# A four-layer gated stack on one core: layer 0's value product in fp32 over centred values, biases added by two-row matmuls, high parts written by ScalarE

## The reference

```python
x = x + tanh(g_xattn[0]) * L0_xattn(layernorm(x), ctx, ctx)   # 8 heads of 16, decay gates
x = x + tanh(g_ffn[0])   * L0_ffn(layernorm(x))               # 8 experts, top 2, capacity 320
x = x + tanh(g_xattn[1]) * (layernorm(x) @ W1.T + mean(ctx) @ W2.T + b)
x = x + tanh(g_ffn[1])   * L1_ffn(layernorm(x))               # rounded to 16 and 4 bits
x = x + tanh(g_xattn[2]) * L2_xattn(layernorm(x), ctx)        # two attentions, 16 heads of 8
x = x + tanh(g_ffn[2])   * L2_ffn(layernorm(x))               # 8 experts, top 2
x = x + tanh(g_xattn[3]) * L3_xattn(layernorm(x), ctx)        # one attention, 16 heads of 8
x = x + tanh(g_ffn[3])   * L3_ffn(layernorm(x))               # 8 experts and a shared one
```

```python
# L0_xattn, per head (16 columns)
C      = (q @ k.T) * exp(D - max_d) / 4
H      = (C @ v) / (max(|sum(C)|, exp(-max_d)) + 1e-6)
out    = (H - mean(H)) / sqrt(var(H) + 1e-5) * gn_w + gn_b     # mean and var over the head's 16
# L2_xattn: x is the normalised input, c the context
a = ln(x + relu(mha1(x, x, x) @ Wo1 + bo1)) * g1 + b1          # causal
c = ln(2 * relu(mha2(ctx, ctx, a) @ Wo2 + bo2)) * g2 + b2
y = ln(c + relu(c @ Wf + bf)) * g3 + b3
```

## Time and profile before

| | us |
|---|---|
| median of 3 runs | 606.84 (605.1 to 607.8) |
| the profiled execution, its own time | 607.42 |
| its span | 605.5 |
| DVE busy | 461.4 |
| PE busy | 420.0 |
| ACT busy | 308.2 |
| POOL busy | 234.4 |

### The profile page before, as it was taken

The page is one execution under the profiler, slowest core; times in us unless marked ns, Lnnn a source line. Parts: engine busy times, 40 slices in busy tenths (PEclk is TensorE's granted clock), DMA queues, the critical chain, the costliest instruction groups (busy, mean ns, idle before and its releaser), DMA issues.

```text
span 605.5 us, 11360 instructions
## 1 busy us (share of the span) xinstructions
PE 420.0 (69%) x4079; PEld 273.0 (45%) x4079; DVE 461.4 (76%) x1305; ACT 308.2 (51%) x596; POOL 234.4 (39%) x358
## 2 busy tenths in 40 slices
PE   2575341258999548103999978776589997878895
PEld 2543220135666433002556656554255664666532
DVE  5559999875667875687978888999878679796742
ACT  2476652227555323732556736762456554757641
POOL 4527775629557670631110111135355572121100
PEclk9999655559999867656999978976799998796988
DMA  7830000450000000000000000000000000000000
GB/s 222 172 32 2 1 1 0 157 122 2 2 1 1 2 0 1 1 0 1 1 2 2 2 1 2 2 2 1 1 2 1 2 0 3 1 2 2 1 17 18
DMA packets 26838, 11.86 MB, mean 20 GB/s; under 512 B 16056, under 2 KB 23712, under 8 KB 26784
## 3 DMA queue, kind: packets, MB, share of 16 engines
q1 hardware_dynamic: 26784, 11.14, 7.4%
HBM read 10.61 MB, written 0.52 MB: 18 GB/s over the span
## 4 chain that ended last, share of the span: by engine, by line
DVE 43%; PE 39%; POOL 6%; issue 6%; ACT 5%; DMA 1%; SPq 1%; DVEq 0%; ACTq 0%
PE psum L653 10%; PE psum L818 6%; DVE qs L1614 5%; PE psum L803 3%; PE psum L804 3%; PE psum L805 3%; DVE stats L1192 3%; DVE z L1200 2%; POOL work L614 2%; PE psum L990 2%; DVE at L1503 1%; DVE mv L1194 1%; PE psum L926 1%; PE psum L930 1%; DVE split L1364 1%
## 5 line engine op out<-in xcount | busy, mean ns | idle before, releaser
L536 POOL TENSOR_SCALAR vr<-mv 128x1 f32<-128x1 f32 x88 | 19.4, 220 | 217.6 <-DVE mv L1194 217.3
L614 POOL TENSOR_TENSOR work<-work 128x512 f16<-128x512 f32 x64 | 72.6, 1162 | 43.2 <-ACT work L1066 43.2
L1614 DVE TENSOR_REDUCE qs<-psum 128x4 f16<-128x512 f32 x96 | 59.6, 689 | 6.0 <-PE psum L905 5.8
L1008 ACT ACTIVATE phase<-psum 128x1024 f16<-128x1024 f16 (+1 forms) x52 | 47.5, 928 | 30.5 <-PE psum L891 15.2
L1491 DVE TENSOR_TENSOR work<-work,psum 128x512 f32<-128x512 f32 x64 | 42.9, 685 | 20.3 <-ACT work L1112 19.8
L1112 ACT ACTIVATE work<-psum 128x512 f32<-128x512 f32 x64 | 37.5, 594 | 37.2 <-PE psum L805 34.5
L1153 ACT ACTIVATE phase<-psum 128x512 f32<-128x512 f32 x96 | 49.8, 601 | 9.5 <-PE psum L930 8.8
L538 POOL TENSOR_TENSOR rstd<-vr,mhalf 128x1 f32<-128x1 f32 x88 | 50.1, 570 | 7.3
L803 PE MATMUL psum<-zTh,split 128*128 128x512 f16 x128 | 51.1, 399 | 1.9 <-DVE work L1491 1.5
L818 PE MATMUL psum<-wout,work 128*128 128x128 f16 x768 | 48.9, 223 | 3.3 <-POOL work L614 1.8
L804 PE MATMUL psum<-zTl,split 128*128 128x512 f16 x128 | 51.0, 398 | 0.0
(11 more groups left out here) (347 smaller groups left out, 1040.1 us busy)
## 6 DMA issues: line engine op xcount, KB each, us to landing
stage_f<-in_L_ffn_W_in SPq DMA_DIRECT2D x1, 2048.0 KB, 10.0
stage_f<-in_L_ffn_w SPq DMA_DIRECT2D x1, 2048.0 KB, 8.4
x<-in_x SPq DMA_DIRECT2D x1, 512.0 KB, 4.1
c<-in_ctx SPq DMA_DIRECT2D x1, 512.0 KB, 5.5
...
```

The costliest lines, as they stand in the source:

```text
L614: ch.do(pool.tensor_tensor(hidl[:, n % 2, k, :], act[:, n % 2, k, :], hidh[:, n % 2, k, :], ALU.subtract), sem("hid_low"))
L1008: ch.do(A(out, view(u), ACT.Copy), banks.freed(stage, b, name))
L1614: ch.do(v.tensor_reduce(groups(qs[:, b, :, 3 * DA:3 * DA + 1], 4)[:, j], u, AX.X, ALU.max, negate=True), free_of(stage, b, f"s{j}"))
```

## The change

- **Layer 0.** Stage x0_cut is gone. dec stays in fp32 and is the moving operand; the values are the weights of the matmul, 32 columns for a head, in fp32, with the mean over each head's 16 columns taken off before (cm). x0_value now gives the result transposed; ACT copies it (avT0), PE transposes it back in a new stage x0_back, ACT takes its squares, and DVE has five steps left. The mean needs no step, since the values are centred, and the division by the norm is folded into the power: it is taken of var + 1e-5 * norm^2. POOL adds gn_b (scaled by tanh(g)) to x ahead, so that x0_group has three steps.
- **Biases by matmul.** Eight bias rows are loaded on two partitions (bias32, in the load group "l2"), ACT takes their fp16 high parts in stage w1, POOL makes the two rows of bias16 in stage router, and PE opens an accumulation with minus16 (all -1) times bias16 (add_bias): in x1_out, c_kv, b_q, a_wo, b_wo and b_f. A b_q bias comes from b1 times Wq2, in w1, and g1 is multiplied into Wq2, so that a_norm is the plain normalising step.
- **High parts on ScalarE.** In m_kv and b_q, ACT writes both high parts and the values; DVE writes the low parts alone (low).
- **Norms.** b_norm and b_last are two steps (affine). POOL adds b3 and bo (scaled) to x behind x2_z and x3_z.
- **Loads.** 7 rows on 128 partitions in the place of 13, none for bq, bk and bv; in "l2" come seven loads on two partitions, g1 and b1 twice.

```diff
-    "x0": ["x0_split", "x0_stack", "x0_score", "x0_cut", "x0_value", "x0_group", "f0_z", "f0_t"],
+    "x0": ["x0_split", "x0_stack", "x0_score", "x0_value", "x0_back", "x0_group", "f0_z", "f0_t"],
-    "x0_split": 12.8, "x0_stack": 13.8, "x0_score": 14.8, "x0_cut": 15.8, "x0_value": 16.8, "x0_group": 17.8,
+    "x0_split": 12.8, "x0_stack": 13.8, "x0_score": 14.8, "x0_value": 15.8, "x0_back": 16.8, "x0_group": 17.8,
-    "setup": ["ctx0", "ctx1", "gate_w"], "w1": ["u"], "w8": ["u"], "router": ["u"],
+    "setup": ["ctx0", "ctx1", "gate_w"], "w1": ["u", "bq"], "w8": ["u"], "router": ["u"],
...
@@ POOL @@
-                    ch.do(pool.tensor_tensor(v0[:, b, :, D0 + 1:2 * D0 + 1], cb, kk[:, :, 0:D0], ALU.subtract), sem("v0_ready"))
-                elif stage == "x0_cut":
...
+                    if b == 0:
+                        pool.wait_ge(sem("cm_ready"), 1)
+                    ch.do(pool.tensor_tensor(v0[:, b, 0:H0 * n0].rearrange("p (h d) -> p h d", h=H0)[:, :, 0:D0], cb,
+                                             bc(cm[:, b * H0:(b + 1) * H0].unsqueeze(2), [P, H0, D0]), ALU.subtract), sem("v0_ready"))
...
+                    ch.do(pool.tensor_tensor(x[:, b, :], x[:, b, :], vec("L0_xattn_gn_b"), ALU.add), sem("x_biased"))
...
+                elif stage == "router":
+                    loaded(pool, "rows")
+                    pool.wait_ge(sem("tg_ready"), 1)
+                    for name, k in (("L2_xattn_g3", 2), ("L2_xattn_b3", 2), ("L3_xattn_bo", 3)):
+                        ch.do(pool.tensor_scalar(rows_of(name), rows_of(name), tg[:, k:k + 1], None, ALU.mult),
+                              sem("rows_scaled") if k == 3 else None)
+
+                    pool.wait_ge(sem("bias_high"), 1)
+                    ch.do(pool.tensor_scalar(bias16[:, :, :], bias16[:, :, :], ident[0:2, 1:2], None, ALU.mult))
+                    ch.sync()
+                    ch.do(pool.tensor_tensor(bias16[:, :, :], bias16[:, :, :], bias32, ALU.subtract), sem("bias_ready"))
+                    ch.do(pool.tensor_scalar(wB[:, 0, :], wB[:, 0, :], g1c[:, :], None, ALU.mult), sem("wq_scaled"))
@@ PE @@
+            def add_bias(out, first, n=1):
+
+                return mm_(out, minus16[:, :], bias16[:, first:first + n, :].rearrange("p i d -> p (i d)"), start=True, stop=False)
...
-                    for h in range(H0):
-                        mm_(u[:, h * n:(h + 1) * n], ch0[:, b % 2, h, :], v0[:, b, h, :], start=True, stop=False)
-                        last = mm_(u[:, h * n:h * n + D0 + 1], cl0[:, b % 2, h, :], v0[:, b, h, 0:D0 + 1], start=False, stop=True)
+                    for g in range(2):
+                        banks.emptied(pe, "x0_score", b, f"s{g}")
+                        for j in range(4):
+                            h = 2 * j + g
+                            last = one(u[32 * j:32 * j + SLOTA, g * P:(g + 1) * P], v0[:, b, h * n0:h * n0 + SLOTA], dec[:, b % 2, g, j, :])
+                    banks.fill(last, stage, b, "u")
+                elif stage == "x0_back":
+                    banks.emptied(pe, "x0_value", b, "u")
+                    u = banks.take(pe, stage, b, "u")
+                    for g in range(2):
+                        last = tr(u[:, g * P:(g + 1) * P], avT0[:, b % 2, g, :], ident[:, :])
@@ ACT @@
+                    u = banks.get(act_, stage, b, "bq")
+                    ch.do(A(bias32[:, 7, :], u[0:2, 0:D], ACT.Copy), banks.freed(stage, b, "bq"))
+                    act_.wait_ge(*banks.freed(stage, b, "bq"))
+                    loaded(act_, "l2")
+                    ch.do(A(bias16[:, :, :], bias32, ACT.Copy), sem("bias_high"))
...
+                elif stage in ("a_kv", "b_kv", "c_kv"):
...
+                    if m != "b":
+                        twice(qs[:, b, :, 0:2 * DA].rearrange("p h (s d) -> p h s d", d=DA), heads(u[:, 0:D]))
+                    twice(ks[:, b, :, 0:4 * DA].rearrange("p h (s d) -> p h s d", d=DA)[:, :, 0:3:2, :], heads(u[:, D:2 * D]))
+                    ch.do(A(vA[:, b, :, 0:DA], heads(u[:, 2 * D:3 * D]), ACT.Copy), sem(m + "_kv_high"))
@@ DVE @@
+            def affine(stage, out, src, b, tmp, gain, plus, signal):
+
+                dve.wait_ge(sem("rstd_ready"), norm_turn[NORM_OF[stage], b])
+                ch.do(stt(tmp, src, mv[:, b, 0:1], gain, ALU.subtract, ALU.mult))
+                ch.sync()
+                ch.do(stt(out, tmp, rstd[:, b:b + 1], plus, ALU.mult, ALU.add), signal)
...
+                elif stage == "x0_gate":
+                    if b == NB - 1:
+                        ch.do(v.tensor_reduce(cm[:, :], c[:, :, :].rearrange("p b (h d) -> p (b h) d", d=D0), AX.X, ALU.add))
...
-                        ch.do(tt(w, u[:, 0:3 * D].rearrange("p (i d) -> p i d", i=3), bqkv[:, :, :], ALU.add), f)
...
+                    dve.wait_ge(sem(m + "_kv_high"), b + 1)
+                    u = banks.tile(stage, b, "qkv")
+                    if m != "b":
+                        low(b, u[:, 0:D], 0)
+                    low(b, u[:, D:2 * D], 1, free_of(stage, b, "qkv"))
```

More of the change, by code:

```diff
@@ L680, in _ @@
                     banks.fill(last, stage, b, "u")
+                    loaded(pe, "l2")
+                    u = banks.take(pe, stage, b, "bq")
+                    banks.fill(one(u[0:2, 0:D], b1c[:, :], wB[:, 0, :]), stage, b, "bq")
                 elif stage == "w8":
@@ L872, in _ @@
                     pe.wait_ge(sem("a_out" if stage == "b_qt" else "b_out"), b + 1)
+                    if stage == "b_qt" and b == 0:
+                        pe.wait_ge(sem("wq_scaled"), 1)
                     u = banks.take(pe, stage, b, "t")
@@ L957, in _ @@
                     u = banks.take(pe, stage, b, "wo")
-                    banks.fill(one(u[:, 0:D], atT[m + "_wt"][:, :], {"a": woA, "b": woB, "c": woC}[m][:, :]), stage, b, "wo")
+                    if m == "c":
+                        last = one(u[:, 0:D], atT["c_wt"][:, :], woC[:, :])
+                    else:
+                        add_bias(u[:, 0:D], {"a": 1, "b": 2}[m])
+                        last = plus(u[:, 0:D], atT[m + "_wt"][:, :], {"a": woA, "b": woB}[m][:, :])
+                    banks.fill(last, stage, b, "wo")
                 elif stage == "b_f":
@@ L961, in _ @@
                     u = banks.take(pe, stage, b, "f")
-                    banks.fill(one(u[:, 0:D], atT["b_ft"][:, :], wf[:, :]), stage, b, "f")
+                    add_bias(u[:, 0:D], 3)
+                    banks.fill(plus(u[:, 0:D], atT["b_ft"][:, :], wf[:, :]), stage, b, "f")
                 elif stage == "f3_up":
@@ L1003, in _, with heads, twice @@
             A = nc.scalar.activation
+            def heads(src):
+                return src.rearrange("p (h d) -> p h d", h=HA)
+            def twice(out, src, signal=None):
+                ch.do(A(out, bc(src.unsqueeze(2), [P, HA, 2, DA]), ACT.Copy), signal)
             def copy_free(stage, b, name, out, view):
@@ L1045, in _ @@
                         if f == "f2":
-                            for j in range(2):
-                                act_.wait_ge(sem(f"cl0_ready_{j}"), NB)
+                            banks.filled(act_, "x0_value", NB - 1, "u")
                     if f == "f0":
@@ L1080, in _ @@
                 elif stage == "x0_score":
-                    for j in range(2):
-                        if b >= 2:
-                            act_.wait_ge(sem(f"cl0_ready_{j}"), b - 1)
-                        u = banks.get(act_, stage, b, f"e{j}")
-                        ch.do(A(dec[:, b % 2, j, :, :], u.rearrange("p (h q) -> p h q", h=4), ACT.Exp), banks.freed(stage, b, f"e{j}"))
-                elif stage == "x0_cut":
                     if b >= 2:
```

219 lines of the change are left out of this document (101 added, 118 removed), and 2 rows, old and new, of the table UNITS.

## The result

The changed kernel took **579.8 us** (median of 4 runs, 578.9 to 580.8) beside 606.5 for the kernel before (605.1 to 607.8): a ratio of 0.955, 95% interval 0.953 to 0.958. The prediction was 575, with a range of 553 to 594. The span of the profiled execution fell from 605.5 to 578.8 us, by 26.7.

The account below looks back on a forecast made before the run. DVE was taken as the bound in layer 0 and layer 2's second part, PE from 299 to 348 us. Terms 17.5 - 7.4 + 1.5 + 14 + 6 = 31.6 us off 607.42, less 0.58, gave 575 us, range 562 to 588 (8 in 10: 553 to 594).

Parts of the forecast that it names:

- the slots: Sign in layer 0's attention: score products every 6.5 to 7.3 us, where a slot took 9.3 us before.
- Layer 0, 17.5 us: Layer 0: 17.5 us gained, mostly from DVE work removed, as 12 + 2 + 5.3 - 1.1 - 0.7.
- the coupled 8.2: Layer 0's upper slot estimate: 8.2 us if x0_back's wait for POOL's power and ACT steps is all exposed.
- Router, 7.4 lost: Router stage: added POOL steps ahead of layer 0's third low-part pair make PE wait, 7.4 us lost (4.6 to 7.6).
- all of it shows: Router stage: PE, the bound behind POOL's added steps, has only two more up products meanwhile; 7.4 us lost.
- rival C: Layer 2, 299 to 348 us: new hops break up PE's work, clock granted at 1.2 GHz; 623 us, chance 5%.
- Layer 1, 1.5 gained: Layer 1: x1_out loses eight DVE bias adds, 2.3 us, half under DVE; 1.5 us gained.
- Layer 2, 14 gained: Layer 2: DVE loses 21.2 us from 348 to 452 us, PE is late next; 14 us gained.
- the later bound fills the stretch as DVE did: Layer 2, 348 to 452 us: PE's 78 us fill 87% of the stretch, making it 90 us, 14 gained.
- Layer 3, 6 gained: Layer 3: DVE loses 16 us, PE was as full, a bit over a third pays; 6 us gained (3 to 12).
- A: Coupling: engines wait for each other where DVE leaves, layer 0 slots 8.2 us; 593 us, chance 20%.
- B: DVE's removed work pays in full across layers 0 to 3, 61.4 us gained; 546 us, chance 17%.

Follow-up runs that it names:

- e10: Changed kernel with router's POOL steps in gaps, multiply in two operations, x0_back's bank copied by ACT, column means behind the fourth x0_norm: 567.3 us, ratio 0.936.
- e2: Changed kernel with every tensor_scalar of stage router written with two operations in place of one: one run, span 576.1 us against 578.8.
- e1: Changed kernel with the six POOL steps of stage router moved early, beside layer 0's routing: 575.5 us, ratio 0.947.
- e7: Changed kernel with router's POOL multiply and subtraction in gaps between low parts, the rest where POOL is idle: 574.0 us, ratio 0.947.
- e9: Changed kernel with only the norms of layer 2's attentions given back their old number of DVE steps, 40 more: ratio 0.967 to the kernel before.
- e12: Changed kernel with high parts, values, biases bo1, bo2, bf and norm steps of layer 2 on DVE as before: ratio 0.974 to the kernel before.
- e4: Changed kernel with high parts and values of layers 2 and 3 back from ACT to DVE, bias matmuls kept: ratio 0.958 to the kernel before.
- e5: Changed kernel with layer 2's biases bo1, bo2 and bf added by DVE again, their 24 matmuls gone: ratio 0.958 to the kernel before.
- e6: Changed kernel with high parts and values of layers 2 and 3, and biases bo1, bo2, bf, all on DVE again: ratio 0.960 to the kernel before.
- e8: Changed kernel with ACT copying x0_back's result out of PSUM, so its bank is freed before x0_group: ratio 0.955 to the kernel before.

## Why the prediction was right, and where it was not

The total was right (575 against 579.8, inside the forecast's own 562 to 588), partly by luck: terms missed in opposite directions. By the marks the 26.7 us are 21.9 gained in layer 0's attention, 10.1 lost by the router stage, and gained again 0.9 in the rest of layer 0's experts, 0.6 in layer 1, 8.8 in layer 2 and 4.6 in layer 3. Of the signs named, DVE's busy time (75 us down) and PE's share in layer 2's second part (86% from 342 to 446 us) came; the slots (6.3 us against 6.5 to 7.3), POOL's 1024 columns (2.83 against 3 or more) and PE's wait (7.73 against 4 to 7) lay a little outside.

- **Layer 0, 17.5 us.** 21.9 by the first down product. The slots went from 9.3 to 6.3 us over the last five (15.2 us in the place of 12), the two before them gave 2.0 as said, and what stands behind the last product 6.5 in the place of 5.3. The mechanism was right: the time went to 6.3, between DVE's own 5.2 and the coupled 8.2. (The middle of these two is 6.7, not the 6.9 that I took for it; that made the term 1 us too small.) What I took as one loop were two kinds of slot, 4.9 us where POOL has no weight cuts, up to 7.5 where it has. The head cost 2.1, not 1.1, and e10 gave it back; the ACT work in w1 showed no cost (0.4 gained in the place of 0.7 lost). That it was the work taken off DVE which gave the 21.9 us is read from the two traces; no run puts the steps of layer 0 back, so how they divide between the cut and the other steps is not shown.
- **Router, 7.4 lost.** The added wait was 7.4 us as priced by L638, with parts that missed both ways (2.83 for 3.4, 0.60 for 0.45 four times, 2.13 for 2.4; and the 3.4 should have been L638's 3.6). e2 shows the reason why L638 was the right row, the single-operation form. The step that failed is "all of it shows" as the whole price: behind the wait PE ran at 1.2 GHz, 2.7 us more. "In the meantime two more up products" had PE idle for 7.7 us, and the clock belonged to rival C in my list and nowhere else. The whole stage cost 10.1 us, which e1 and e7 gave back.
- **Layer 1, 1.5 gained.** 0.6.
- **Layer 2, 14 gained.** 8.8 (2.7, 3.2 and 2.9). This was the weakest term, and its form was wrong. I took the stretch 348 to 452 as one, with "the later bound fills the stretch as DVE did". Up to the last b_max PE was at 90 of 101 us before the change already, so 21 us less of DVE gave 2.7. The other 6.1 came behind it. Of the 8.8 the norm steps carry 5.7 (e9), and with all DVE steps back 7.4 are gone (e12). The high parts and values, a good part of the 21.2 us, gave nothing by themselves that stands out of the scatter (e4). A bias matmul was sized at 0.1 us in the place of 0.233, but e5 says that this wasn't it.
- **Layer 3, 6 gained.** 4.6, with 5.4 of it ahead of the second half's update. There the four c_kv had stood on DVE in front of the experts' sums: bias, casts and low parts of one of them took 3.4 us from 498.20 us on, and the last down product took 2.72 us (at 515.82), as at the slower clock; in the changed kernel it took 1.50 (489.51). How much of this is the bias and how much the casts no run settles: with the casts back and the bias still on PE, e4 and e12 lose 0.7 of the 5.4, and e6, whose trace is of its slowest run, 1.8.

**The rivals.** *A* exists and was small: PE waited for the loop in four slots, not in every one (in the kernel's order of banks x0_back of the sixth batch follows on x0_value, since a unit of f0_t stands between). Cutting it gave 3.7 us (e8), while A was 18 us from the forecast, 6.5 of them in layer 0. The ACT hop of layer 2 cost nothing that shows (e4 is not faster). *B* is out: in layer 2 up to the last b_max 21 us less of DVE gave 2.7, under a PE that was nearly full. *C* is out in its place (granted clock 1.00 from 278.8 to 319 us), but its mechanism stood 150 us earlier.
